# First attention: GpSimd takes the products of exponents and chunk weights from VectorE

## The reference, cut to what matters

```python
kc = k.reshape(B, NH, C, SPLIT, HD)
vc = v.reshape(B, NH, C, SPLIT, HD)
scores = jnp.einsum('bhqd,bhckd->bhcqk', q, kc) * scale
w = jax.nn.softmax(scores.astype(jnp.float32), axis=-1).astype(q.dtype)
chunk_out = jnp.einsum('bhcqk,bhckd->bhcqd', w, vc)
sum_w = w.sum(axis=-1, keepdims=True)
combined = (chunk_out * sum_w).sum(axis=2)
total = sum_w.sum(axis=2)
out = combined / (total + 1e-09)
```

## Time and profile before

| | us |
|---|---|
| median of 3 runs | 2272.51 (2267.11 to 2275.48) |
| profiled execution | 2269.63 |
| its span | 2267.8 |
| TensorE busy | 1984.8 (88%) |
| VectorE busy | 1444.2 (64%) |
| ScalarE busy | 971.0 (43%) |
| GpSimd busy | 572.7 (25%) |

### The profile page before, as it was taken

The page is one execution under the profiler, slowest core; times in us unless marked ns, Lnnn a source line. Parts: engine busy times, 40 slices in busy tenths (PEclk is TensorE's granted clock), DMA queues, the critical chain, the costliest instruction groups (busy, mean ns, idle before and its releaser), DMA issues.

```text
span 2267.8 us, 31835 instructions
## 1 busy us (share of the span) xinstructions
PE 1984.8 (88%) x10080; PEld 1175.0 (52%) x10080; DVE 1444.2 (64%) x2432; ACT 971.0 (43%) x1358; POOL 572.7 (25%) x543
## 2 busy tenths in 40 slices
PE   6899999996996999997768999999969889999975
PEld 3444444443783555556544444444448755555554
DVE  5678777866417776852366787778662377776432
ACT  2445444441224566551234444444413156656411
POOL 0000000000001687884120000000000037797931
PEclk7899999998887999997969999999979879999977
DMA  2366666678000000000514666666760000000015
GB/s 92 80 142 147 143 148 143 143 163 237 21 1 10 1 10 6 1 1 29 159 33 102 144 148 146 154 151 151 167 203 1 1 10 10 2 6 1 1 61 148
DMA packets 84846, 187.99 MB, mean 83 GB/s; under 512 B 17697, under 2 KB 46754, under 8 KB 83106
## 3 DMA queue, kind: packets, MB, share of 16 engines
q1 hardware_dynamic: 83650, 183.76, 32.3%
q0 software_dynamic: 1024, 2.10, 0.3%
HBM read 178.47 MB, written 8.91 MB: 83 GB/s over the span
## 4 chain that ended last, share of the span: by engine, by line
PE 61%; DVE 16%; issue 11%; ACT 6%; DMA 3%; SPq 1%; POOL 1%; DVEq 0%; ACTq 0%; POOLq 0%
PE PS L794 9%; PE PS L766 5%; PE PS L730 5%; PE PS L905 3%; PE PS L945 3%; PE PS L965 3%; DVE mx L1837 3%; PE PS L751 3%; PE PS L756 3%; PE PS L1136 3%; PE PS L948 2%; PE PS L860 2%; PE PS L1191 2%; DMA V<-weight_rows 2%; DVE mrow L1971 2%
## 5 line engine op out<-in xcount | busy, mean ns | idle before, releaser
L1837 DVE TENSOR_REDUCE mx<-PS 128x8 f32<-128x512 f32 x512 | 330.5, 685 | 181.8 <-PE PS L730 170.4
L2337 POOL TENSOR_TENSOR Esum<-Esum,EE 128x512 f32<-128x512 f32 (+3 forms) x320 | 337.5, 1084 | 16.5 <-POOL Esum L2337 10.1
L1866 DVE TENSOR_TENSOR EE<-EE,V 128x1024 f32<-128x1024 f32 x256 | 302.8, 1218 | 45.9 <-DMA V<-weight_rows 45.5
L1457 ACT ACTIVATE EE<-PS 128x1024 f32<-128x1024 f32 x256 | 260.3, 1025 | 143.3 <-PE PS L756 141.4
L2291 POOL TENSOR_TENSOR U<-xn,norm_aff 128x1024 f32<-128x1024 f32 x2 | 4.7, 2356 | 1084.0 <-DVE QA L2262 1084.0
L794 PE MATMUL PS<-EE,Vlater 128*64 128x512 f32 x1024 | 251.9, 611 | 9.1 <-ACT U L1423 8.3
L1971 DVE TENSOR_REDUCE mrow<-PS 128x1 f32<-128x512 f32 (+3 forms) x384 | 203.0, 551 | 86.7 <-PE PS L908 67.4
L730 PE MATMUL PS<-KA,QA 128*128 128x512 f32 x512 | 204.6, 451 | 33.9 <-DVE mx L1837 24.4
L751 PE MATMUL PS<-QA,KA 128*128 128x512 f32 x512 | 184.9, 442 | 0.0
L1541 ACT ACTIVATE EE<-PS 128x1024 f32<-128x1024 f32 (+2 forms) x192 | 137.8, 738 | 105.8 <-PE PS L948 103.8
L730 PEld LDWEIGHTS PS<-KA,QA 128*128 128x128 f32 x512 | 97.3, 195 | 132.8 <-DVE mx L1837 88.5
(11 more groups left out here) (306 smaller groups left out, 3310.3 us busy)
## 6 DMA issues: line engine op xcount, KB each, us to landing
V<-weight_rows SPq DMA_DIRECT2D x512, 256.0 KB, 5.5
EE<-in_w SPq DMA_DIRECT2D x48, 192.0 KB, 2.7
V<-in_Wg SPq DMA_DIRECT2D x4, 1024.0 KB, 6.3
EE<-in_Wu SPq DMA_DIRECT2D x4, 1024.0 KB, 11.4
EE<-in_Wd SPq DMA_DIRECT2D x4, 1024.0 KB, 13.4
sorted_out<-U SPq DMA_DIRECT2D x12, 256.0 KB, 3.1
wo<-in_wo SPq DMA_DIRECT2D x5, 512.0 KB, 3.9
wq_s<-in_wq SPq DMA_DIRECT2D x17, 128.0 KB, 2.9
```

Source lines behind the costliest of these rows:

```text
L1457: act.activation(EE[i % 2][:, t, :], banks(2 * (t % 2)), ACT.Exp, scale=QSCALE).then_inc(s["p2_exp"], 1)
L1837: dve.tensor_reduce(mx[:, t, half * 8:half * 8 + 8], banks(5 + x % 2, BANK).rearrange("p (c k) -> p c k", c=8), AX, ALU.max).then_inc(s["p ...
L1866: dve.tensor_tensor(EE[i % 2][:, t, :], EE[i % 2][:, t, :], weight_ring[a % 2][:, odd, :], ALU.mult).then_inc(p3_mul, 1)
L2337: ins = pool.tensor_tensor(Esum[:, h, lo:hi], Esum[:, h, lo:hi], e_tile(t)[:, h, lo - t * P:hi - t * P], ALU.add)
```

## The change

VectorE's `weigh` and all its calls go, those behind the last head too. GpSimd gets one loop over all heads and tiles between its copy of x and its work for the mixture. It waits for the slot's weights, multiplies in place, and raises `p3_mul`. The waits of all other engines, the ring, its loads and the order on TensorE, ScalarE and SP stay as they are.

```diff
-                def weigh(i, t):
-
-                    a, odd = divmod(t, 2)
-                    dve.wait_ge(wt_in[t % 4], ((h0 + i) * 2 + t // 4 + 1) * 32)
-                    dve.tensor_tensor(EE[i % 2][:, t, :], EE[i % 2][:, t, :], weight_ring[a % 2][:, odd, :],
-                                      ALU.mult).then_inc(p3_mul, 1)
...
-                        for k in range(2):
-                            if t % 2 and t >= 5 and i >= 1:
-                                weigh(i - 1, t - 5 + k)
-                            if t % 2 and t < 5 and i >= 2:
-                                weigh(i - 2, t + 3 + k)
...
-                for t in range(4, NT):
-                    weigh(i - 1, t)
-                for t in range(NT):
-                    weigh(i, t)
...
                 pool.tensor_copy(x[:, :, :], x_next).then_inc(s_xc, 1)
+                for i in range(HEADS):
+                    for t in range(NT):
+                        pool.wait_ge(wt_in[t % 4], ((b * HEADS + i) * 2 + t // 4 + 1) * 32)
+                        pool.sem_inc(s_held, 1)
+                        pool.tensor_tensor(EE[i % 2][:, t, :], EE[i % 2][:, t, :], weight_ring[t // 2 % 2][:, t % 2, :],
+                                           ALU.mult).then_inc(p3_mul, 1)
                 pool.wait_ge(xf_low, b + 1)
```

## The result

| | before | after |
|---|---|---|
| median, same chip | 2272.59 us (4 runs) | 2353.28 us (2349.65 to 2356.05, 4 runs) |
| ratio | | 1.0357 [1.0332, 1.0382] |
| profiled execution, its span | 2269.63, 2267.8 us | 2354.69, 2352.8 us |
| TensorE, VectorE, GpSimd busy | 1984.8, 1444.2, 572.7 us | 2019.1, 1231.2, 1172.4 us |

The change makes the kernel 3.6% slower, 80.7 us. The forecast was slower by 40 us, with a range up to 2345: the direction was right, and the size was half of what came. Two executions stand far apart from all others of their kernel (3159.29 us in e7_best and 3715.3 us in a later series of the kernel before) and enter no ratio.

What follows compares the result with a forecast made beforehand. TensorE was taken to bound the stage, VectorE second. Added waits and tails less VectorE's relief gave 19.3 us in batch 0 and 20.2 in batch 1, together 39.5 over 2272.5: 2312 us, range 2278 to 2345.

Steps and rivals of the forecast that it cites:

- VectorE's relief in ordinary heads: Removing VectorE's products is worth nothing in an ordinary head, since VectorE idles or TensorE waits for ScalarE anyway.
- Head 1: Head 1 of each batch: without queued products TensorE's 3.16 us wait shrinks; 4.4 us less in batch 0, 3.5 in batch 1.
- GpSimd's rate: GpSimd's products take 2.3 us each, ends 2.18 and 2.6, hidden in ordinary heads.
- Rival 3: GpSimd becomes the bound from 3.6 us per product on; at 4.0 us the time is 2360 us; chance 0.07.
- rival 2: No wait in the normaliser, VectorE only relieved: about 6 us less, 2266 to 2267 us; chance 0.14.
- L1849 held, one for one into TensorE's gap: Normaliser, heads 2 to 15: L1849 waits 1.15 us for GpSimd's instruction, delaying maxima and TensorE at tile 1; 16 us per batch.
- L1854: Normaliser's tensor_scalar: half the rest of a GpSimd instruction taken as wait; upper end some 3 us per batch more than none.
- rival 1: The clock falls at the new tile 1 stall, near 2.46 us, in half of 28 heads: 20 us more, 2332 us; chance 0.10.
- The tail: End of each batch: 0.75 us at head 15's tile 1, 4.7 for the last normaliser, 1.1 for the last eight products.
- Head 13: Four slot-normalising tensor_scalars of head 13 run while GpSimd works: 0 to 3 us, 1 taken per batch.
- the prediction's high end: 28 x 2.1 us for L1849, all waits of L1854 and 2.6 us per product: +80.5 us, 2353 us.

Runs made afterwards that it cites:

- e7_best: e1's normaliser; GpSimd's products only in heads 0 to 13, VectorE's in 14 and 15; head 13's slot tensor_scalars moved to tiles 2 and 3: 2261.6 us, ratio 0.9969.
- e1: Changed kernel with VectorE's normaliser writing sw, r1 and tot to PSUM, so no product reads two SBUF tensors; GpSimd's products stay: 2278.87 us, ratio 1.0029 to before.
- e3: Changed kernel with each GpSimd product cut into two of 512 columns, back to back: 2387.09 us, ratio 1.0495.
- e4b: e1 plus two VectorE reductions of 0.68 us each behind the second product, in every head: 2332.59 us, ratio 1.028.
- e6: Changed kernel with products in halves of 512 columns, GpSimd waiting for each half's own semaphore before the next: 2309.23 us, ratio 1.0194.

## Why the prediction was right in its mechanism and wrong in its size

- **VectorE's relief in ordinary heads: nothing.** Right: in e1, where nothing is held, the distances between transposes are 28.9 and 29.7 us as before.
- **Head 1.** Right. The stall of 3.16 us and the slow stretch behind it are gone:

```profile
100.32 1.04 PE L737 MATMUL PS<-consts,mx 128*16 128x128 f32 x8 [0.22 <-DVE mx L1837]
...
103.20 1.08 PE L794 MATMUL PS<-EE,Vlater 128*64 128x512 f32 x4 [0.83 <-POOL EE L2277]
```

  The distance fell by 2.24 us in batch 0, and it holds 1.31 us of the first held normaliser and 1.13 us of waiting for L1858, so the relief was 4.7 us; 4.4 was forecast. In batch 1 the same working gives about 3.2; 3.5 was forecast.
- **GpSimd's rate: 2.3 us taken, 2.38 measured.** Near enough, and hidden in ordinary heads as forecast. Rival 3 is dead, and so is rival 2, by the median of L1849 (1766 ns).
- **L1849 held, one for one into TensorE's gap: right.** The size was 1.15 us per head, half an instruction. It was 1.44 (34.5 us in 24 heads): some 7 us short. Batch 0 gave 16.0 us in 13 gaps, 1.23 each; batch 1 gave 21.1. The three longest holds are all in batch 1 (1429.17, 1461.96 and 1560.99, 2.2 to 2.8 us). One of them is a thing that the prediction didn't have, L1849 passed over for a second product, 2.3 us; the other two are the unlucky end of its phase. Why they fall into batch 1 was not settled.
- **L1854.** It waits, as its upper end had it (median 912 ns, alone 161). The Trainium skill (GPSIMD Engine Reference, Key points) names VectorE's two-port modes beside two SBUF inputs as what contends with GpSimd. The trace agrees in so far as L1854, with one SBUF input, is held; no run shows which mode it runs in. The prediction also said that holding through a whole instruction comes from the rows alone. The Trainium skill has it on another page, which the prediction had not drawn on: SBUF — State Buffer, section "SBUF: two separate sides", calls the shared ports an exclusive lock for the whole instruction. The 0.96 us held at 336.26 agree; the 2.8 us at 1461.96 and the 5.2 us of e3 go beyond it.
- **The step that failed: the stall was costed at its own length.** "It delays the maxima behind it and TensorE's wait at tile 1 one for one" was true and incomplete. Behind such a wait the granted clock fell in 17 of 26 heads, and L794 alone lost 24 us (table above). The prediction knew this as rival 1, gave it a chance of 0.10 and kept it out of the sum. Two readings of rows made it small. It asked for a gap near 2.46 us, since a gap of 1.40 at 508.38 passed without harm, where the runs show falls behind gaps of 1.25 (307.07) and 1.73 (e4b). And it took the fall as another outcome, to be weighed, when every longer gap draws on the same mechanism. With rival 1's own 20 us in the sum the forecast would have been 2332, and 21 us short.
- **The tail.** 16.2 us forecast, 20.9 measured. It isn't the last normaliser: L783 behind it waited 7.03 us (553.97) and 3.15 us (1718.81), 1.66 in both batches before, so it added 6.9 us in all where 4.7 per batch, 9.4, were forecast. The transposes of head 15, which did not wait before, waited 2.93 us (525.62) and 2.99 us (1694.85), 5.9 where about 3 were forecast, since L1854 was held there too. And the low clock behind 525.62 and 553.97 took some 3.6 us, which the sum didn't have.
- **Head 13.** 1 us per batch for the held tensor_scalars; L737 waited 1.92 us at 482.72, and in e1 a slow group of L794 stood behind the same wait (454.45).

Had the low clock of those 24 heads been in the sum (24), the gaps at 1.44 (7) and the tails at what they were (5), the forecast's 39.5 would have been some 75, near the 83 measured in the two stages. That the prediction's high end came to 2353, the measured time, is chance: it had 2.1 us per gap and the slowest rate everywhere, and no clock. What is left is in matmuls of other lines within the slow stretches, and in head 13.

## What to carry to other kernels

Work moved to GpSimd can cost next to nothing by itself (e1 is 0.3% over the kernel before) and yet be paid for by a VectorE instruction of 0.28 us that reads two SBUF tensors on the critical path. Before the move, list each such VectorE instruction beside the new work, give it a PSUM operand if one is free, and, where GpSimd's instructions are short and follow each other at once, leave gaps between them. When a new stall lands on TensorE, put the clock in the sum, not among the rivals: here each microsecond of stall cost 0.7 more.

## What the runs showed of the hardware that was not expected

- An unbroken row of short GpSimd instructions can hold VectorE to the end of the row (17 of 29 held L1849 in e3, 7.0 us at most), and 0.08 to 0.20 us between them were enough to let it in each time (1.35 us at most in e6). A row of products twice as long passed it over at one end of 22 only. Without gaps the short instructions cost 34 us more than the long ones.
- One operand in PSUM makes the same product immune: 289 to 290 ns in all 32 cases beside a GpSimd at work, with the result in PSUM; L1863, whose result goes to SBUF, keeps 291 to 292 too. That the one-input tensor_scalar of e1 on PSUM was not held either (165 to 175 ns) fits.
- TensorE's granted clock fell to 0.62 behind a gap of 1.25 us in one head (306.04), and L794 kept its 1.94 us behind 2.48 us in another (1400.61) of the same kernel; at one length, 1.72 to 1.76 us, it fell in 18 of 26 heads.
